# Attention inside a transformer layer on one core: queries in the column halves for P times V, output tiles projected two at a time in row halves, scaling on ScalarE, adding on GpSimd, keys loaded once a head

## Time and profile before

| | us |
|---|---|
| median of 3 runs | 3310.79 (3310.57 to 3320.97) |
| the profiled execution, its own time | 3305.17 |
| span of the profile | 3303.7 |
| `attend`, from its first score to the end | 800.8 to 3303.7 |

### The profile page before, as it was taken

One profiled execution on the slowest core, in us unless ns is written; L12 is line 12 of the kernel. 1 busy time (PEld: TensorE's weight loads), 2 busy tenths in 40 slices (PEclk: granted clock), 3 DMA queues, 4 the chain that ended last, 5 costly groups with the idle time before them and its releaser, 6 DMA issues.

```text
span 3303.7 us, 53774 instructions
## 1 busy us (share of the span) xinstructions
PE 3196.1 (97%) x14468; PEld 1707.0 (52%) x14468; DVE 2766.0 (84%) x3431; ACT 1767.6 (54%) x3013; POOL 1120.0 (34%) x1347
## 2 busy tenths in 40 slices
PE   7799999898899999999999999999999999999998
PEld 3355444555455555555555555555555555555554
DVE  7612444234999999999999999999999999999996
ACT  4312320344666666666666666666666666666663
POOL 4677770012554555555544444444000000000000
PEclk9899999998999999999999999999999999999999
DMA  8623886665999999999999999999999888889887
GB/s 300 265 70 117 310 268 153 223 228 169 250 257 251 265 250 258 247 258 254 257 257 255 253 256 255 255 252 274 253 228 229 221 229 228 233 228 229 226 224 184
DMA packets 348745, 777.70 MB, mean 235 GB/s; under 512 B 130541, under 2 KB 182520, under 8 KB 340112
## 3 DMA queue, kind: packets, MB, share of 16 engines
q1 hardware_dynamic: 315664, 708.30, 79.0%
q0 software_dynamic: 33024, 68.71, 7.8%
HBM read 238.22 MB, written 161.61 MB: 121 GB/s over the span
## 4 chain that ended last, share of the span: by engine, by line
DVE 38%; PE 28%; issue 6%; DMA 2%; SPq 2%; DVEq 1%; ACT 0%
DVE at_half_max L1136 21%; DVE at_blocks L1152 14%; PE at_ps L1028 11%; PE at_ps L1058 9%; PE at_ps L1041 4%; PE at_ps L1072 3%; DMA at_moved<-at_blocks 2%; SPq L919 2%; DVE at_acc_second L1178 1%; DVE at_acc L1178 1%; DVE at_neg_max L1141 1%; DVEq L34 1%; DVE at_total L1188 0%; DVE ahead_xe L1178 0%; DVE at_inv L1191 0%
## 5 line engine op out<-in xcount | busy, mean ns | idle before, releaser
L1108 ACT ACTIVATE at_prob<-at_ps,at_neg_max 128x1024 f32<-128x1024 f32 x1024 | 1145.0, 1118 | 903.1 <-DVE at_neg_max L1141 788.7
L1136 DVE TENSOR_REDUCE at_half_max<-at_ps 128x1 f32<-128x1024 f32 x1024 | 1205.9, 1219 | 10.2 <-PE at_ps L1028 7.3
L1152 DVE STREAM_TRANSPOSE at_blocks<-at_prob 128x1536 f32<-128x1536 f32 x512 | 905.5, 1769 | 0.3 <-DMA at_moved<-at_blocks 0.3
L1028 PE MATMUL at_ps<-ahead_k_hl,ahead_q_hh 128*128 128x512 f32 x2048 | 850.5, 415 | 17.2 <-ACT at_prob L1108 10.3
L1028 PE MATMUL at_ps<-ahead_k_hl,ahead_q_ll 128*128 128x512 f32 x2048 | 806.4, 394 | 0.0
L1058 PE MATMUL at_ps<-at_moved,at_v 128*64 128x512 f32 x3072 | 726.3, 593 | 8.3 <-DMA at_moved<-at_blocks 7.0
L1041 PEld LDWEIGHTS at_ps<-keep_ident,at_prob 128*128 128x128 f32 x2048 | 215.8, 141 | 436.6 <-DVE at_acc_second L1178 170.8
L1028 PEld LDWEIGHTS at_ps<-ahead_k_hl,ahead_q_hh 128*128 128x128 f32 x2048 | 387.3, 189 | 87.4 <-ACT at_prob L1108 15.1
L1028 PEld LDWEIGHTS at_ps<-ahead_k_hl,ahead_q_ll 128*128 128x128 f32 x2048 | 388.1, 190 | 67.4
L980 POOL TENSOR_SCALAR ahead_gu<-ahead_gu,at_g_gain 128x256 f32<-128x256 f32 x256 | 236.6, 924 | 453.1 <-DMA ahead_gu<-ye,at_g_index 413.5
L1058 PEld LDWEIGHTS at_ps<-at_moved,at_v 128*64 128x64 f32 x3072 | 220.4, 137 | 286.3 <-issue 220.4
(11 more groups left out here) (119 smaller groups left out, 2287.4 us busy)
## 6 DMA issues: line engine op xcount, KB each, us to landing
at_moved<-at_blocks SPq DMA_DIRECT2D x2048, 192.0 KB
ahead_k_hl<-k_parts SPq DMA_DIRECT2D x64, 1024.0 KB, 8.2
ahead_q_hh<-q_parts SPq DMA_DIRECT2D x128, 256.0 KB
ahead_q_ll<-q_parts SPq DMA_DIRECT2D x128, 256.0 KB
xbuf<-pr_zeros SPq DMA_DIRECT2D x32, 512.0 KB, 5.1
q_parts<-pr_part_hi SPq DMA_DIRECT2D x64, 256.0 KB
q_parts<-pr_part_lo SPq DMA_DIRECT2D x64, 256.0 KB
k_parts<-pr_part_hi SPq DMA_DIRECT2D x64, 256.0 KB, 2.2
```

The lines of the kernel that those rows point to most:

```text
L1028: last = nc.tensor.matmul(ps[:, bank, :], q[:, g % 2, j * P:(j + 1) * P], k_hl[:, side, c * CH:(c + 1) * CH], start=first, stop=not first)
L1108: nc.scalar.activation(prob[:, i % 2, half * 1024:(half + 1) * 1024], ps[:, banks[0]:banks[1], :].rearrange("p b c -> p (b c)"), ACT.Exp, ...
L1136: nc.vector.tensor_reduce(half_max[:, i % 2, half:half + 1], ps[:, banks[0]:banks[1], :], AX.XY, ALU.max).then_inc(max_step, 1)
L1152: nc.vector.transpose(blocks[:, parity, :, j, :, :].rearrange("p c t k -> p t c k"), prob[:, (s["s"] - 1) % 2, 0:MOVED * P].rearrange("p ( ...
```

## The change

P times V now keeps all keys of a tile in one matmul and splits the *queries*: the first two query tiles of the group go to the left 64 columns of the array, the last two to the right. The result is complete in each half, 256 columns wide, and takes twice as many matmuls of half the length. A projection contracts over 64 rows only, so two tiles are projected together, one from the upper and one from the lower row half, into banks 0 and 1 (the even tiles' early banks), in every second slot (the odd ones). PE's order becomes scores, projection, transposes, product with V. ACT scales the two projected tiles first, then does `take`, then both exponentials. DVE has neither the scaling nor the adding; POOL adds the scaled tile (now in SBUF) to one accumulator that serves both batches and starts from `base`. The gathering is spread over all heads, one token tile a head: 8 gathers in slots 0 to 7, 8 multiplications and additions in slots 8 to 15. Keys are loaded once a head, in two transfers of half size, into one of two buffers; W_O once a head too. Loops run over pairs of heads. In the diff, what only renames is left out.

```diff
-def load_k(sp, scr, start, b, h, side):
-    sp.dma_start(start["k_hl"][:, side, :].bitcast(F32), scr["k"][bass.ds(h * P, P), b * T:(b + 1) * T]
...
+def load_k(sp, scr, start, b, h, side, part):
+    keys = slice(part * T // 2, (part + 1) * T // 2)
+    sp.dma_start(start["k_hl"][:, side, keys].bitcast(F32),
...
-PV_ORDER = (3, 0, 1, 2)
+GQ = GT // 2
+PV_PLACES = ((12, 16), (0, 4), (4, 8), (8, 12))
...
             def score(s, half):
...
                     wait_pos(pe, early_exp, tile - 1)
+                    wait_pos(pe, scaled, s["projected"])
...
             def transpose(s):
                 tile = s["tile"] - 2
                 pe.wait_ge(late_exp, tile + 1)
                 wait_pos(pe, copied, tile)
-                if s["out"]:
-                    wait_pos(pe, added, s["out"][0] * GT + s["out"][2])
...
             def times_v(s):
-                for j in range(GT):
-                    t = quarter * GT + j
-                    side = t % 2 * DH
-                    p_T = moved[:, parity, :, :, t, :] if t < MOVED else turned_sb[:, parity, t - MOVED, :, :, :]
-                    last = nc.tensor.matmul(ps[side:side + DH, PV_BANK, :], v[:, t, :], p_T,
+                for t in tiles:
+                    for half in range(2):
+                        side, queries = half * DH, slice(half * GQ, (half + 1) * GQ)
+                        p_T = (moved[:, parity, :, queries, t, :] if t < MOVED else
+                               turned_sb[:, parity, t - MOVED, :, queries, :])
+                        last = nc.tensor.matmul(ps[side:side + DH, PV_BANK, 0:GQ * P], v[:, t, :], p_T,
...
             def project(s):
-                wait_pos(pe, added, n)
-                for side in (0, DH):
-                    last = nc.tensor.matmul(ps[side:side + DH, TURN_BANK, 0:D],
-                                            oT[:, g % 2, j * P + side:j * P + side + DH], wo[:, g // 2, :],
+                for n, g, j, half, behind in s["out"]:
+                    if half == 0:
+                        pe.wait_ge(early_exp, min(s["s"], TILES) + s["head"] * TILES)
+                        wait_pos(pe, scaled, n)
+                    rows, queries = slice(half * DH, (half + 1) * DH), slice(j % GQ * P, (j % GQ + 1) * P)
+                    nc.tensor.matmul(out_of(s, half), oT[rows, g % 2, queries], wo[rows, s["out_side"], :],
+                                     start=True, stop=True).then_inc(projected, 1)
 
             def body(b, h, s):
-                if s["late"]:
-                    transpose(s)
                 if s["scores"]:
                     score(s, 0)
                     score(s, 1)
-                if s["out"]:
-                    project(s)
+                project(s)
+                if s["late"]:
+                    transpose(s)
                 if s["pv"]:
                     times_v(s)
...
+            def scale_out(s):
+                for n, g, j, half, _ in s["out"]:
+                    act.wait_ge(projected, n + 1)
...
+                    wait_pos(act, added, n - GT + 1)
+                    nc.scalar.activation(scaled_sb[:, j, :], out_of(s, half), ACT.Identity, scale=inv[:, t:t + 1]
+                                         ).then_inc(scaled, 1)
...
             def body(b, h, s):
+                scale_out(s)
+                if s["late"]:
+                    take(s)
                 if s["scores"]:
                     exponent(s, 1)
-                if s["turn"]:
-                    take(s)
-                if s["scores"]:
                     exponent(s, 0)
...
         def _(dve):
-                    nc.vector.memset(acc_first[:, :, :], 0.0)
-                    nc.vector.memset(acc_last, 0.0).then_inc(cleared, 1)
...
-                    nc.vector.scalar_tensor_tensor(out=acc(of, t), in0=ps[:, TURN_BANK, 0:D], scalar=inv[:, t:t + 1],
-                                                   in1=acc(of, t), op0=ALU.mult, op1=ALU.add
-                                                   ).then_inc(added, 1)
...
         def _(pool):
+            def routed(b, s):
+                k, h, n = s["s"] % K, s["h"], s["head"]
+                part = k // (K // 2)
+                if s["s"] < K:
...
+                    nc.gpsimd.indirect_dma_start(
+                        out=row(k), out_offset=None, in_=scr["ye"][:, :],
...
+                    return
+                if k % (K // 2) == 0:
+                    wait_apart(pool, gathered[part], n * 64 + 64, pool_waits)
+                nc.gpsimd.tensor_scalar(row(k), row(k), g_gain[:, k:k + 1], None, ALU.mult).then_inc(g_scaled, 1)
+                nc.gpsimd.tensor_tensor(into, into, row(k), ALU.add).then_inc(g_added, 1)
...
+                for n, g, j, half, behind in s["out"]:
+                    wait_apart(pool, scaled, n + 1, pool_waits)
+                    nc.gpsimd.tensor_tensor(acc[:, t, :], acc[:, t, :], scaled_sb[:, j, :], ALU.add
+                                            ).then_inc(added, 1)
```

More of the change, by code:

```diff
@@ L630, in load @@
                     load_expert(sp, io, scr, ahead, e, q)
-            load_k(sp, scr, start, 0, 0, 0)
+            for part in range(2):
+                load_k(sp, scr, start, 0, 0, 0, part)
             load_q(sp, scr, start, 0, 0, 0)
@@ L811, in attend @@
         g_gain = m.sb("g_gain", [P, K])
-        rows = ahead["gu"][:, :, :, :].rearrange("p q k o -> p (q k) o")
-        rest = m.sb("rest", [P, D])
-        rest_t = rows[:, 0:2, :]
+        rows_first = ahead["gu"][:, :, :, :].rearrange("p q k o -> p (q k) o")
+        rows_last = ahead["xe"][:, 1, :, :]
+        scaled_sb = m.sb("scaled", [P, GT, D])
         v_loaded = m.sems("v_loaded", GT)
@@ L864, in slots @@
                 out = not opens or s >= OUT_LAG
+                place = (s - OUT_LAG) % GT
                 yield dict(
-                    s=s, head=head, tile=tile, scores=s < TILES,
+                    s=s, h=h, head=head, tile=tile, scores=s < TILES, side=side, pair=pair,
+                    out_side=1 - side if s < OUT_LAG else side, out_pair=pair - 1 if s < OUT_LAG and not side else pair,
                     turn=(head * GROUPS + back[0], back[0] % 2, (s - 1) % GT) if turn and s <= TILES else None,
+                    taken=(head * GROUPS + (s - 2) // GT, (s - 2) // GT % 2, (s - 2) % GT),
                     late=(not opens or s >= 2) and s <= TILES + 1,
@@ L870, in slots @@
                     if pv and s < PV_LAG + TILES else None,
-                    out=(head * GROUPS + back[2], back[2] % GROUPS, (s - OUT_LAG) % GT, s < OUT_LAG)
-                    if out and s < OUT_LAG + TILES else None)
+                    pv_group=head * GROUPS + back[2] + 1, projected=head * TILES + back[2] * GT + (0, GQ, GQ, GT)[place],
+                    out=[(head * TILES + back[2] * GT + place + half, back[2] % GROUPS, place // 2 + half * GQ, half,
+                          s < OUT_LAG) for half in range(2)]
+                    if out and place % 2 == 0 and s < OUT_LAG + TILES else ())
         def over_heads(eng, body):
@@ L877, in over_heads, with out_of @@
                     body(b, 0, s)
-                with eng.Fori(1, H - 1) as h:
-                    for s in slots(b, h):
-                        body(b, h, s)
+                with eng.Fori(0, H // 2 - 1) as i:
+                    for u in (1, 2):
+                        for s in slots(b, (i, u)):
+                            body(b, (i, u), s)
                 for s in slots(b, H - 1):
                     body(b, H - 1, s)
+        def out_of(s, half):
+            return ps[:, EARLY[(s["s"] + 1) % 2][0] + half, 0:D]
         def exchanges(head, g):
@@ L957, in _ @@
         def _(pool):
[L958 to L982, removed]
-                        nc.gpsimd.tensor_tensor(rest[:, :], rest[:, :], rows[:, k, :], ALU.add).then_inc(g_step, 1)
-                        wait_apart(pool, g_step, i * (2 * K) + 8 * r + 2 * k + 2, pool_waits)
@@ L1010, in _ @@
+            over_heads(pool, body)
         @block.tensor
@@ L1046, in times_v @@
                 group, g, place = s["pv"]
-                quarter, parity = PV_ORDER[place], g % 2
+                parity = g % 2
+                tiles = range(*PV_PLACES[place])
                 if place == 0:
@@ new lines, in times_v @@
+                for t in tiles:
[4 more added lines that the diff above has]
+                        last = nc.tensor.matmul(ps[side:side + DH, PV_BANK, 0:GQ * P], v[:, t, :], p_T,
+                                                start=(place == 0 and t == tiles[0]),
+                                                stop=(place == GT - 1 and t == tiles[-1]))
```

189 lines of the change are left out of this document (93 added, 96 removed).

## The result

The changed kernel takes 3343.5 us (median of 5), against 3310.8 before: ratio 1.0094, 95% interval 1.008 to 1.0109. Slower by 0.9%, where 3244 and "faster" were forecast. The time is inside the stated range by luck: the direction is wrong, and the range reaches this far only for the two rivals that end near 3350, neither of which is what happened.

The account below looks back on a forecast made before the run. PE and DVE were both taken as full (4.73 of a 4.813 us slot); relieving DVE leaves PE at 4.685. That saves 65 us over 511 slots plus 2 at the start, from 3310.8 to 3244, range 3170 to 3350.

Parts of the forecast that it names:

- the two rivals that end near 3350: Rival 3 (3356) and rival 4 (3353), both slower on PE, chance 0.12 each.
- The sum for PE without the jumps: PE's mean attention slot after the change: even 4.30, odd 5.03, plus 0.02 for V's loads, 4.685 us.
- the change between array modes: PE switching between whole array and halves: 0.09 in, 0.15 back, 0.24 us more in each odd slot.
- rival 4: Projection's row halves run one after another on PE: odd slot 5.46, mean 4.90, time 3353; chance 0.12.
- rival 3: P times V pays for 16 weight loads a slot instead of 8: slot 4.905, time 3356; chance 0.12.
- rival 2: PE's mode changes cost nothing more, drain hidden or not needed: slot 4.545, time 3172; chance 0.14.
- rival 5: Odd slots' projection waits for the early exponential, say 0.25 late: slot 4.81, time 3309; chance 0.12.
- The 0.13 margin: Early exponential's accumulator read ends at 5.41, PE's projection comes at 5.54: in time by 0.13 us.
- PE as the bound once DVE has slack: In attention slots DVE falls to 4.30, so PE should run through at its own 4.685 us.
- ACT's scaling: Scaling 256 columns on ACT takes about 0.32 us; the late exponential's 0.2 delay is hidden by V.
- POOL, transfers, keys once a head at nothing: POOL's adding and gathering, DMA at 235 GB/s, and halved key loads: no gain, no loss.
- The start: Accumulators' memset no longer stands ahead of the first maxima: 2 us less.

Follow-up runs that it names:

- e2: Changed kernel with loops over single heads instead of pairs, keys and W_O loaded twice a head again: 3268.6 us, ratio 0.9868 to the kernel before.
- e1: Kernel before the change, with only its loops run over pairs of heads: 3398.5 us, ratio 1.0263.
- e9: Kernel before the change, loop over pairs of heads on PE alone, other engines over single heads: ratio 1.0139.
- e4: Changed kernel, pair loops kept, with transposes ahead of the projection on PE and `take` ahead of the scaling on ACT: 3313.5 us, ratio 1.0002.
- e11: Changed kernel with single-head loops, keys and W_O twice a head, and transposes ahead of the projection: 3370.2 us, ratio 0.9717, on a slower chip.
- e6: Kernel before the change without DVE's scaling and adding (L1178); ACT scales into SBUF, nothing adds the tiles: ratio 0.9909.
- e7: Kernel before the change with its loops over heads written out: ratio 0.9907, by the medians 37 us less on its chip.
- e3: Changed kernel with its loops written out, keys still loaded once a head: 3277.1 us, ratio 0.9899.
- e8: Kernel of e2 with its loops written out, keys and W_O twice a head: 3454.3 us, ratio 0.9812, on a slower chip.
- e10: Kernel before the change, loops over pairs of heads on all engines but PE: ratio 1.0124.

## Why the prediction was wrong, point by point

- **The step that failed** is the line in the change's costs that isn't there. "Loops run over pairs of heads" stands in the description of the change and got neither a price nor a rival. It is worth (4.892 - 4.756) x 511 = 70 us of the trace, 75 in time (e2), or about 6 a jump: a stall of 4.2 on the mean, late engines behind it, and scores at half the clock. With it undone the change is faster, as forecast in kind: 3269. The Trainium skill, "Runtime: NRT & Kernel Launch", section Instruction fetch mechanics, says that a taken branch whose target is out of the fetched window waits for a transfer, and gives PE room for 2048 instructions and other engines for 512, in blocks of 16 KiB. The runs agree with the stall, and with the blocks for PE; q14's packets are of 8 KB. From one jump back to the next the trace has 867 records of PE (matmuls, weight loads, waits, register operations) in one head before, 1050 after, 2100 in a pair after; the last is past the Trainium skill's 2048, and it is fetched again on each pass in both loops. But PE's pair of heads in e1 and e9 has 1732, which is under it, and is fetched again in the first batch all the same, and DVE's pair in e1 has 362, under the 512, and is fetched again in the second. So that a jump back to a long body is what costs is shown; how long a body may be is not.
- **The sum for PE without the jumps** was 4.685, measured 4.756 (e2): 36 us too little. The term that was mis-sized is the change between array modes, 0.24 per round trip. Transposes take 0.52 up to V in even slots and 0.59 behind a projection, where 0.50 (0.41 + 0.09) was put; scores behind V take 1.96 to the transposes where 1.93 was put. In the earlier trace rows the scores stand behind the transposes, never behind V, and the transposes never between the scores and V or behind a projection, so neither could be read there.
- **The projection's row halves** do run side by side (rival 4 falls): 0.63 from projection to transposes, where 0.49 + 0.15 was forecast. **V** takes 1.87 to 1.88 with the change behind it, where 1.86 + 0.02 was: rival 3 falls, and here the measurement decides against the rule of the Trainium skill, "TensorE: Matmul & The Clock Gate", Part 3: Packing small matmuls, that loads overlap only where the row group differs: V's 16 loads, 1.49 us of them in the slot shown, stand within the 1.88 of its matmuls.
- **The additional change between modes** (rival 2's question) is real: e4 takes one away and the odd slot loses 0.15. The rule of the Trainium skill, "TensorEngine Tiling (Array Packing)", Key Properties, that a change of mode drains the engine agrees, and the runs have it between row and column halves too.
- **The wait for the early exponential** (rival 5) is there in name, 117 times, but the projection starts 0.32 after the last score, as V does in the earlier trace rows without such a wait: nothing lost. The 0.13 margin was enough.
- **PE as the bound once DVE has slack**: right. In e2 and e11 the mean slots, 4.756 and 4.681, are what the PE timelines add up to (4.75, and 4.68 in e4), with DVE's idle time ended by PE's scores. That DVE's relief alone is worth little fits e6 (33 us, where (4.813 - 4.73) x 511 = 42 was the most by the first chip's slots), but e7 keeps its share open.
- **ACT's scaling** takes 0.47, where 0.32 was put. It stayed hidden, as said: no wait of PE for it stands in the waits over 900 to 3200 us. The groups of ACT by line, over 900 to 3200 us (busy us, mean ns, idle before):

```profile
L1117 ACT COPY at_turned_sb<-at_ps 128x512 f32<-128x512 f32 x468 | 274.4, 586 | 385.5 <-PE at_ps L1062 384.1 <-issue 1.5
...
L1142 ACT ACTIVATE at_scaled<-at_ps,at_inv 128x256 f32<-128x256 f32 x468 | 196.5, 471 | 237.9 <-PE at_ps L1096 237.9
```

- **POOL, transfers, keys once a head at nothing**: right. DMA stands at 0.88 and 220 GB/s, and e3 against e8 shows 0.005 a slot for the keys. The start gained 1.4 from the memset (first score to first L1141 or L1173: 6.5 before, 5.1 after) where 2 was put. Another 5.2 us come from a first score at 795.6 in place of 800.8, ahead of all that the sum had; why is not shown, and e4, with the same start, has its first L1173 3 us later (803.7).

## What to carry to other kernels

A loop's body is a resource of its own: before unrolling by two to get fixed buffer sides, count the body's instructions per engine and look in the profile's instruction queues for fetches that stop once the loop runs. If they don't stop, each jump back cost about 6 us here and 7 in e1; write the loop out instead, or keep the body short and pay for the other thing (here a second load of keys, which was free). On TensorE, put instructions with the same array mode beside one another: a change costs here about 0.15 us on the way back and 0.09 on the way in.

## What the runs showed of the hardware that was not expected

- A jump back behind which instructions are fetched again stops PE for 3.5 to 5.6 us (e1, e4, the changed kernel) and DVE for 3.5 to 5.8 (e1, e10), and in the changed kernel the granted clock behind PE's 4.3 us of standing still is 0.50 in the next windows, from 1498 to 1502 us.
- Instructions that run straight on are fetched in time, 135 packets of 16 KB without a stall of PE (e3).
- Two matmuls of 64 rows run side by side in row halves, four records in 0.63 with the change of mode behind them, into two banks.
- ScalarE's 128x256 activation with a scale per partition takes 471 ns from PSUM, against 586 for a copy of 512 columns.
